# One core, eight-expert FFN and causal attention: projections of the third group moved behind the fourth step's scores, and outputs placed inside short steps and two steps behind near the end

## The reference

```python
x = x + 0.5 * ffn(layernorm(x))           # all 8 experts for every token, y scaled by a gate
x = x + attention(layernorm(x) * w + b)   # 8 heads of 8, l2-normalised q and k, scale 8, causal softmax, w_out
x = x + 0.5 * ffn(layernorm(x))
# ffn: h = gelu(x @ w1[e] + b1[e]); y = sum over e of h @ w2[e]; hidden 256 per expert
```

## Time and profile before

| what | value |
|---|---|
| median of 3 runs | 274.77 us (274.76 to 275.49) |
| the profiled execution | 274.75 us |
| its span, first to last instruction | 273.0 us |
| PE busy | 264.0 us (97%) |
| DVE busy | 221.0 us (81%) |
| ACT busy | 220.9 us (81%) |
| POOL busy | 76.3 us (28%) |
| granted TensorE clock | 0.999 of full |

### The profile page before, as it was taken

The page is one execution under the profiler, slowest core; times in us unless marked ns, Lnnn a source line. Parts: engine busy times, 40 slices in busy tenths (PEclk is TensorE's granted clock), DMA queues, the critical chain, the costliest instruction groups (busy, mean ns, idle before and its releaser), DMA issues.

```text
span 273.0 us, 4939 instructions
## 1 busy us (share of the span) xinstructions
PE 264.0 (97%) x1621; PEld 183.0 (67%) x1621; DVE 221.0 (81%) x599; ACT 220.9 (81%) x345; POOL 76.3 (28%) x146
## 2 busy tenths in 40 slices
PE   8999999999999999889998999999999999999995
PEld 7876878887888787323333432278887887888783
DVE  8999899989898979966687355588889798688784
ACT  2897678778877788899999999977677868769673
POOL 6202204124840592352247333600400200200100
PEclk9999999999999999999999999999999999999999
DMA  4830000000000000000000000330004210300311
GB/s 147 239 98 4 0 1 2 1 0 0 2 1 0 5 0 0 2 0 2 1 2 0 4 0 2 83 74 0 1 0 116 42 38 19 62 10 29 79 38 38
DMA packets 21660, 7.80 MB, mean 29 GB/s; under 512 B 13474, under 2 KB 20868, under 8 KB 21636
## 3 DMA queue, kind: packets, MB, share of 16 engines
q1 hardware_dynamic: 21492, 7.43, 10.6%
q10 hardware_dynamic: 144, 0.07, 0.1%
HBM read 4.88 MB, written 2.62 MB: 27 GB/s over the span
## 4 chain that ended last, share of the span: by engine, by line
PE 81%; ACT 7%; DVE 6%; issue 5%; POOL 0%; DVEq 0%; ACTq 0%; POOLq 0%
PE ps L528 10%; PE ps L546 10%; PE ps L551 10%; PE ps L549 10%; PE ps L534 9%; PE ps L531 9%; PE ps L682 9%; ACT probs L864 4%; PE ps L659 4%; PE ps L721 2%; PE ps L713 2%; DVE h_lo L1026 2%; PE ps L627 2%; ACT h L851 1%; PE ps L637 1%
## 5 line engine op out<-in xcount | busy, mean ns | idle before, releaser
L851 ACT ACTIVATE h<-ps,cols 128x512 f32<-128x512 f32 x128 | 87.9, 694 | 36.8 <-PE ps L534 33.3
L1026 DVE TENSOR_TENSOR h_lo<-h,h_hi 128x512 fp32r<-128x512 f32 x128 | 88.1, 694 | 15.3 <-ACT h_hi L854 12.6
L864 ACT ACTIVATE probs<-ps 128x1024 f32<-128x1024 f32 (+1 forms) x80 | 67.3, 1008 | 1.6 <-PE ps L659 1.4
L528 PE MATMUL ps<-xT_hi,w_hi 128*128 128x512 f32 x128 | 51.7, 404 | 0.0
L546 PE MATMUL ps<-h_hi,w_hi 128*128 128x512 f32 x128 | 50.7, 396 | 0.3 <-ACT yT L876 0.3
L551 PE MATMUL ps<-h_lo,w_hi 128*128 128x512 f32 x128 | 50.2, 392 | 0.0
L854 ACT ACTIVATE h_hi<-ps,cols 128x512 fp32r<-128x512 f32 x73 | 50.2, 688 | 0.0
L534 PE MATMUL ps<-xT_lo,w_hi 128*128 128x512 f32 x128 | 50.0, 390 | 0.0
L531 PE MATMUL ps<-xT_hi,w_lo 128*128 128x512 f32 x128 | 49.9, 390 | 0.0
L549 PE MATMUL ps<-h_hi,w_lo 128*128 128x512 f32 x128 | 49.8, 389 | 0.0
L682 PE MATMUL ps<-probs,v_ones 128*32 128x512 f32 (+3 forms) x384 | 38.8, 495 | 0.3 <-POOL probs L1463 0.2
(11 more groups left out here) (146 smaller groups left out, 268.4 us busy)
## 6 DMA issues: line engine op xcount, KB each, us to landing
w_raw<-in_L_ffn_w SPq DMA_DIRECT2D x8, 256.0 KB, 4.4
turned<-blocks SPq DMA_DIRECT2D x6, 256.0 KB, 2.2
w_raw<-turned SPq DMA_DIRECT2D x24, 64.0 KB, 2.4
x_sb<-in_L_attn_x SPq DMA_DIRECT2D x3, 256.0 KB, 6.6
out_x<-x_sb SPq DMA_DIRECT2D x3, 256.0 KB, 2.3
x_sb<-in_L_attn_x SPq DMA_DIRECT2D x2, 128.0 KB, 2.1
wout_sb<-in_L_attn_w_out SPq DMA_DIRECT2D x8, 4.0 KB
out_x<-x_sb SPq DMA_DIRECT2D x1, 128.0 KB, 1.9
```

The lines of the kernel that those rows point to most:

```text
L528: pe.matmul(bank, w1_hi[:, w], xT_hi[:, cols_g], start=True, stop=False)
L851: first = nc.scalar.activation(h[:, slot, :], ps[:, BANK_H + slot, :], ACT.Gelu, bias=bias)
L864: nc.scalar.activation(probs[:, s % P_SLOTS, :, 0:width], ps[:, bank:bank + 2, 0:width], ACT.Exp, scale=SCALE).then_inc(exp_done, 1)
L1026: dve.tensor_tensor(h_lo[:, slot, :], h[:, slot, :], h_hi[:, slot, :].bitcast(f32), ALU.subtract).then_inc(split_done, 1)
```

## The change

- `qkv_products(LAST - 1)` leaves chunk 13 of the last FFN group and is called once after that group, so behind `scores(3)`. It uses banks 6 and 7 in place of 5 and 6, and so also waits for `kT_done` of group 1. For this DVE's `copy_k(1)` moves from chunk 15 to chunk 12, behind `copy_q(1)`.
- ACT's `affine_features(2)` moves from ahead of the table load and `exp_scores(0)` to behind them.
- `scores(4)` no longer waits for `qkv_copied`. The last group's `y_transposes`, which do wait for it, move from ahead of `scores(4)` to behind `scores(5)`.
- DVE's `square_sums(2)` and `guesses(2)` move behind the last group's residual and statistics. POOL's `ln_twice(LAST)` moves from step 5 to step 7.
- In a short quad step the outputs stand between its two scores instead of behind them.
- From k = 35 on outputs run two quad steps behind: k = 35 issues outputs 32 and 33, and after the scores of k = 39 only output 38, the three `up` and output 39 remain.
- The job `q_stack` of the last group moves from output 18 to output 19.

```diff
+PV_CLOSER = 35
-                (q1 + 12, "q_stack", LAST), (q2 + 1, "k_stack", LAST),
+                (q1 + 13, "q_stack", LAST), (q2 + 1, "k_stack", LAST),
+        def pv_until(k):
+            return k + 1 - (PV_LAG if k < PV_CLOSER else PV_LAG - 1)
...
-            return (BANK_LN, BANK_QT) if p == LAST - 1 else (BANK_QT, BANK_KT)
+            return BANK_QT, BANK_KT
...
-                    if operands and g >= 1 and c == at["att_qkv"]:
+                    if operands and 1 <= g < LAST and c == at["att_qkv"]:
                         qkv_products(g - 1)
...
-                if p == LAST - 1:
-                    pe.wait_ge(qT_done, p)
-                else:
-                    pe.wait_ge(gate_logits_done, p + 2)
-                    pe.wait_ge(qT_done, p)
-                    pe.wait_ge(kT_done, p)
+                pe.wait_ge(gate_logits_done, p + 2)
+                pe.wait_ge(qT_done, p)
+                pe.wait_ge(kT_done, p)
...
-                    pe.wait_ge(kT_done, LAST - 1)
+                    pe.wait_ge(qkv_copied, LAST)
...
             pe.wait_ge(wout_in, 16 * HEADS)
+            qkv_products(LAST - 1)
             next_job = 0
-            for k in range(quad_steps + PV_LAG):
...
+            def scores_of(s):
...
+                if s == 4:
+                    pe.wait_ge(resid, GROUP_TILES * LAST)
+                    pe.wait_ge(xf_done[ATT], LAST)
+                    pe.wait_ge(y_evac, GROUPS)
+                    pe.wait_ge(xf_done[FFN], GROUPS)
...
+            def outputs(k):
+                nonlocal next_job
+                for quad in range(max(pv_until(k - 1), 0), pv_until(k)):
+                    if quad == quad_steps - 1:
                         for c in range(LAG):
                             pe.wait_ge(exp_done, len(steps) - 2 + c // 2 + 1)
                             up(1, GROUPS, c, 0)
+                    pv(quad)
+                    if jobs[next_job][0] == quad:
                         fill(next_job)
                         next_job += 1
+            for k in range(quad_steps):
+                short = steps[2 * k]["last"]
+                scores_of(2 * k)
+                if short:
+                    outputs(k)
+                scores_of(2 * k + 1)
+                if not short:
+                    outputs(k)
+                if k == PV_LAG - 1:
+                    y_transposes(LAST, BANK_YT_LAST)
+            outputs(quad_steps)
+            outputs(quad_steps + 1)
...
                         exp_scores(0)
+                        affine_features(g - 1)
...
-                    if operands and g >= 1 and c == at["att_copy"]:
+                    if operands and 1 <= g < LAST and c == at["att_copy"]:
                         affine_features(g - 1)
...
                             copy_q(g - 2)
+                            if last:
+                                copy_k(g - 2)
                     if operands and last and c == CHUNKS - 1:
-                        copy_k(g - 2)
                         copy_qkv(g - 1)
                         own_squares(g - 1)
-                        square_sums(g - 1)
-                        guesses(g - 1)
...
             aggregate(ATT)
+            square_sums(LAST - 1)
+            guesses(LAST - 1)
             inverse_lengths(dve, LAST - 1)
...
-                if s == 5:
+                if s == 7:
                     ln_twice(LAST)
```

More of the change, by code:

```diff
@@ L741, in _ @@
             pe.wait_ge(wout_in, 16 * HEADS)
+            qkv_products(LAST - 1)
             next_job = 0
-            for k in range(quad_steps + PV_LAG):
[L744 to L763, removed]
+            def scores_of(s):
+                st = steps[s]
+                if st["first"] and s % 2 == 0:
+                    p = Q_GROUPS * st["b"] + st["qg"]
+                    if p < GROUPS // 2:
+                        pe.wait_ge(kT_done, p + 1)
+                    else:
+                        pe.wait_ge(job_emptied, job_number["k_stack", p] + 1)
+                if s == 4:
[3 more added lines that the diff above has]
+                    pe.wait_ge(xf_done[FFN], GROUPS)
+                if s >= 4:
+                    scores(s)
+            def outputs(k):
+                nonlocal next_job
+                for quad in range(max(pv_until(k - 1), 0), pv_until(k)):
+                    if quad == quad_steps - 1:
                         for c in range(LAG):
@@ L767, in _ @@
                             up(1, GROUPS, c, 0)
-                    pv(k - PV_LAG)
-                    if jobs[next_job][0] == k - PV_LAG:
+                    pv(quad)
+                    if jobs[next_job][0] == quad:
                         fill(next_job)
                         next_job += 1
+            for k in range(quad_steps):
[10 more added lines that the diff above has]
+            outputs(quad_steps + 1)
             ffn_groups(nc.tensor, 1, lambda g: ffn_group(1, g))
```

## The result

The change makes the kernel slower by 0.22%: ratio 1.0022, 95% interval 1.0014 to 1.0030. The medians are 275.48 us (10 runs, 275.40 to 275.76) against 274.91 (10 runs, 274.73 to 275.49). 275.1 had been forecast, within 274.1 to 275.9, with 0.70 for "within 0.3%". The time lies within both, 0.4 above the forecast. The profiled execution took 275.58 us (span 273.8) against 274.75 (273.0).

A forecast was written before the change was run, and what follows sets the result against it. The prediction took ACT's string of 80 exponentials, with PE nearly as full, to bound the attention, and PE the FFN layers. Its terms, 0.4 + 0.27 + 0.27 + 0.03 - 0.48 - 0.2 = +0.3, gave 275.1 us, range 274.1 to 275.9.

The forecast's parts named there:

- upper bound of +1.8: Whole kernel: the slow end of what the terms' bounds were said to add up to, -0.7 to +1.8 us.
- shifts add up: Attention: a loss at one place is not won back later, because PE shifts with ACT.
- Start, +0.4: Start of the attention: exponential 6 waits behind the y transposes and starts at 113.85 to 113.9, costing 0.4 us.
- k = 12 and 32, +0.27 each: Short quad steps with jobs: scores behind the output make exponential 26 late by 0.27 us, likewise at k = 32.
- output 9 starts 0.11 earlier: Short step k = 12: output 9, moved between the two scores, starts 0.11 us earlier and ends at 129.8.
- k = 19: Short quad step k = 19: the scores come 0.03 us late, a term of +0.03.
- k = 22, -0.48: Job q_stack one output later: scores 44 pass ahead of the stack transposes, gaining one short exponential, 0.48 us.
- End, -0.2: Outputs two behind from k = 35: output 38, waiting for masks, lets the first `up` start 0.2 us earlier.
- The start gains: Rival at the start: y transposes don't hold scores 6, -0.6 in place of +0.4, so 274.1 us; chance 0.14.
- Later stands absorb: Rival: the start's +0.4 vanishes in the stand ahead of exponential 26, so 274.7 us; chance 0.18.
- DVE's backlog: Rival at the start: DVE falls over 2.0 us behind, holding jobs at outputs 6 and 7; 276.1 us, chance 0.08.
- The clock: Rival: PE's clock falls from 2.4 to 1.2 GHz in the 1.3 us stand, so 276.7 us; chance 0.04.

The follow-up runs named there:

- run three: The changed kernel with the whole start as in the kernel before; short steps, lag and q_stack stay as changed: 275.08 us, ratio 1.0005.
- run five: The changed kernel with the last group's y transposes behind scores 6 and 7 instead of ahead of them: 274.68 us, ratio 0.9996.
- six: The changed kernel with DVE's copy of kT (group 1) behind the gate's shift instead of ahead of it: 274.94 us, ratio 1.0000.
- Run one: The changed kernel with the outputs in short quad steps behind both scores again: 274.66 us, ratio 0.9993.
- seven: The changed kernel with y transposes behind scores 7, kT copy behind the gate's shift, outputs inside a short step only at k = 22: 273.36 us, ratio 0.9940.
- run eight: The changed kernel with the edits of seven, and the first three up chunks of layer 1 ahead of output 38: 272.85 us, ratio 0.9924.
- nine: The changed kernel with outputs inside the short step only at k = 22: 274.75 us, ratio 0.9993.
- run ten: The changed kernel with the outputs of the last short step, k = 39, behind both its scores: 275.48 us, ratio 1.0022.
- run four: The changed kernel with the outputs three quad steps behind to the end: 275.54 us, ratio 1.0029.

## Why the prediction was right

- **The number**: of the steps without layer 0, +0.72, the sum had +0.3. Nearly every term came out above its forecast, by 0.04 to 0.11 us each, and only q_stack below, by 0.09. The time still lies in the range because the range was wide, not because the sum was close. The prediction's upper bound of +1.8 is also mis-added: its terms' bounds give +1.5.
- **What bounds the attention, and that shifts add up**: right. The staircase is flat between its steps, and run three carries the later steps unchanged on a lower base. This was the assumption under the whole sum.
- **Start, +0.4**: measured +0.49. Against the chain as predicted, and with layer 0's 0.11 taken off, each link lies within 0.1: tanh 108.42 (108.40), exponential 1 at 108.56 (108.55), projections' end 111.50 (111.5), copies' end 112.83 (112.8), exponential 6 at 113.96 (113.85 to 113.9). The part above the forecast is PE's pick-up behind DVE's last copy, 0.14 (112.94 to 113.08) instead of 0.05. The 0.05 had come from a wait for ACT; behind DVE, already had 0.15 (144.85 + 0.62 = 145.47, to 145.62). What makes the difference was not tried. Runs five and six show both ends of the chain.
- **k = 12 and 32, +0.27 each**: measured +0.36 and +0.37, above the bound of +0.3. The mechanism was right and the term mis-sized. The failing step is "output 9 starts 0.11 earlier". It starts 0.21 us behind the one score group ahead of it (129.30 to 129.51), just as it had started 0.22 behind two (128.71 to 128.93). Taking two of four score matmuls out saved nothing, because the four run side by side (last section). The missing 0.1 us would also account for k = 19, +0.14 instead of +0.03, and k = 25, +0.06 instead of zero; at these two it was not worked out from rows. Run one shows all four to be the order inside the step.
- **k = 22, -0.48**: measured -0.56 to -0.57. In the changed kernel scores 45 were no longer late: ACT had come 0.14 later through k = 19, and so had more time for them. In runs seven to nine, where it had not, exponential 45 stands 0.07, and in every run with the 0.14 it does not. As I read it, a stand carried in from ahead hid a stand of the place itself, the one exception to independence, and a small one; no run has the order at k = 19 alone.
- **End, -0.2**: measured -0.16. That the first `up` is held by output 38 and the masks of step 77, and not by exponential 79, is shown by run ten, and by run eight, which takes the `up` out from behind them. The credit belongs as much to output 36 or 37 standing between the last scores as to the shorter lag (run four).
- **Rivals.** "The start gains" was wrong for this kernel, and its mechanism is real: run five makes it by moving the call. "Later stands absorb" fell with run three. DVE's backlog had more cover than worked out: DVE still stands 1.25 us ahead of `output(0)` (122.66), so the backlog was 0.6 and not 1.3. The squares start 1.8 late, but all else is 0.6 late and not 0.4, the chain from the squares to the normalisation took 0.2 less, and the normalisation 1.1 us instead of 1.5. In the kernel before, POOL's masks ran beside it until 120.47; in the changed one they had ended at 120.04, before it began at 120.29. Whether that is why it took less was not tried. The clock stayed at its upper level, 2.4 GHz, through the stand of 1.24 us, as a row of a table of stretches says, with PE busy 1.86 of 3.10 us and the clock at 1.00:

```profile
111.00:114.10 3.10, 1.86 (x20) 1.08 (x22) 2.34 (x9) 2.08 (x5) 2.35 (x6) 1.00 0.00 0
```

The Trainium skill ("TensorE: Matmul & The Clock Gate", section "What's actually happening") says that the array's clock halves after an idle stretch; the stand of 1.24 us here did not bring that about, and no run here shows the lower level in the attention.

## What to carry to other kernels

When a stage is paced by one engine, write down the start of each of its instructions in both kernels and subtract: flat parts and steps tell at once which edit cost what, and the edits can then be kept or dropped one by one. A call with a wait in it must be judged by what stands behind it in its queue: the projections behind scores 3 gained 1.2 us ahead of two exponentials and lost 1.8 on the tanh and exponential 6, because a DVE copy went ahead of a tiny operation that another engine needed, and because transposes which nobody was in a hurry for went ahead of scores. Splitting a pair to put long work between cost 0.06 to 0.37 us where the engine was full, and won 0.04 in the one place where it would have waited anyway.

## What the runs showed of the hardware

The score matmuls of a quad step run side by side on PE. Each reads 32 rows of its own, and the four of k = 12 in the kernel before start within 0.01 us of each other (128.709 to 128.719 in its trace). So their number does not set what they take of PE's order, and their columns do. Four of 256 columns took 0.22 us until the output behind them started (128.71 to 128.93), two took 0.21 (129.30 to 129.51, and 145.82 to 146.03), and four of 512 columns took 0.32 (130.39 to 130.71 in run one).

Splitting a quad step's four scores in two therefore costs PE time. From scores 24 to output 10 its order was 1.54 us long in the kernel before and in run one (129.17 to 130.71), and 1.64 in the changed kernel (129.30 to 130.94). A small group on PE should be counted by its columns and by what it can run beside, and not by how many matmuls it has.
